# Turning the first norm's rows on VectorE in blocks of 32 by 32 instead of on TensorE

## The chip, the cores and the metric

The kernel runs on one core of one Trainium2 chip. The metric is the device time of one execution in microseconds (us), as the median over runs of the same program.

## What is computed

Batches of 256 rows by 256 features pass through two blocks, each with a residual. Cut to what matters:

```python
# x, ctx: (16, 256, 256); 8 heads of 32
q = layernorm(x); k = v = ctx                       # the "first norm"
pre = 15 * tanh((concat([q, k, v]) @ ifgate_w.T + b) / 15)
i_pre, f_pre = pre[..., :8], pre[..., 8:]
lf = cumsum(log_sigmoid(f_pre))
log_d[t, s] = lf[t] - lf[s] + i_pre[s]  (s <= t);  m = max_s log_d
s_mat = (q @ k.T / sqrt(32)) * exp(log_d - m)
h = s_mat @ v / (max(|sum s_mat|, exp(-m)) + eps);  h = h * rms_scale * gain
x = x + h
z = layernorm(x)                                    # the "second norm"
a = silu(z @ w1.T * s1) * (z @ w2.T * s2)           # 256 -> 1024
a = gelu(a @ h1.T * t1);  a = gelu(a @ h2.T * t2)   # 1024 -> 1024, twice
out = x + a @ w3.T * s3                             # 1024 -> 256
```

All is float32. The kernel writes each activation as a rounded high part plus a low part (`h_hi`, `h_lo`, type fp32r) and multiplies both by the weights, so every product is two matmuls. The same is done with the inputs of the gate product (`keys_hi/lo`, `normed_hi/lo`).

## The kernel before

The 16 batches are worked in 8 pairs; a pair is 512 rows, four tiles of 128. Each engine has its own instruction stream, written out by hand in program order, and the streams meet only at semaphores. The main loop is `batch(i, ...)`, for i = 0 to 7, on TensorE (PE), ScalarE (ACT) and VectorE (DVE). Three pairs are in flight in it: pair i is in the feed-forward block, pair j = i + 1 in the mixing block, and pair g = i + 2 in its first norm and gates. So the steps on g are done in i = 0 to 5.

One step i on PE is `swiglu` (8 groups, m = 0 to 7), hidden layer 0 (L1209/L1210, 8 groups of 16 matmuls of 512 columns), hidden layer 1 (the same) and `project` (64 matmuls of 256 columns). In a hidden layer groups m = 0 and 1 are interleaved over k = 0 to 7, since each k needs its own `lo`; `between_3(k)` runs after the k-th pair of products of layer 1, `after_3(m)` after its group m. For each group ACT does `gelu` (L591, out of PSUM into `work`) and the copy to `h_hi` (L596), and DVE does `lo` (L890), the subtraction that gives `h_lo`. A PE group waits for the gelu of four groups before it, since four PSUM banks go round.

The steps on g, in the order in which they depend on each other:

1. DVE, layer 0, m = 3 and 4: `norm_1_stats`, `norm_rsqrt`, `norm_1_apply` (L693) put the normed rows in `z` (128 partitions x 4 tiles x 256).
2. PE, layer 1, `between_3(3)`: `turn_z(g)`, 8 transposes of 128 x 128 (L1036) from `z` to `ps_a` banks 0 and 1.
3. ACT, ahead of layer 1's gelus: `split_keys(g)`, then `take_zT(g)`, which waits for the transposes and copies PSUM twice: to `zT` (L510) and, rounded, to `normed_hi` (L516).
4. POOL: `split_keys_low` (L457) and `split_normed_low` (L461) write the low parts; the second is `normed_lo = zT - normed_hi`.
5. PE, `after_3(2)`: `gates(g)`, 16 matmuls; it waits for `s_zlo`, the low part.
6. ACT after gelu 2: `take_gate_low` (L520). DVE after `lo` 2: `add_gate_low` (L736, into a part of the tile that the profile names `decay`). ACT after gelu 3: `soft_cap` (L527), then `softplus` (a table load, L535, L537; the next gelu loads its table back).
7. DVE after `lo` 3: `scan_f` (L743, L747); after `lo` 4: `scan_m` (L755, L759, L760, L761).
8. PE, `after_3(7)`, between layer 1 and `project`: `turn_rows(g)` (L1106), two transposes of `rows`, which wait for the last instruction of `scan_m`. ACT copies them out in `take_cols`.

Around them on DVE, for pair j: at the end of layer 0 `take_state`, `take_far` (L807), `take_num` (L819), which waits for `values(j, 1, 1)`, PE's matmuls of `between_3(0)`, then `mix_divide` (L830 to L833); ahead of layer 1's first `lo` come `mix_square` (L839 to L843), `mix_rsqrt`, `residual` and `norm_2_stats`; after `lo` 1 `norm_rsqrt` and `norm_2_apply`. PE turns the second norm's rows in `turn_z2(j)`, `after_3(6)`.

SP issues the loads and stores in order. `load_z(g)` waits for `s_zT` of the pair before; `keep_rows(g)` and `spread_max(g)` wait for `scan_m`. `scores(j, b)` and `read_state(j)` on PE read `zT`.

Of the kernel before, what the change touches and what calls it, by code (L numbers as in the profile page):

```python
# [15 lines left out]
P = 128  # L16
# [10 lines left out]
BACKEND_EPS, RMS_EPS, LN_EPS = 5e-05, 1e-06, 1e-05  # L27
MASKED = 1e30
RSQRT_SEED = 0x5F3759DF

W = 2
PAIRS = BATCH // W
# [39 lines left out]
def build(nc, x, ctx_tok, ctx_t, gate_w, gate_b, outnorm_w, w_cols, scales, w3_s, out):  # L72
    with ExitStack() as stack:
# [157 lines left out]
        def plain(j):  # L231

            return j < W
# [38 lines left out]
        def reuse(eng, semaphore, value):  # L272

            if not (isinstance(value, int) and value <= 0):
                eng.wait_ge(semaphore, value)
# [222 lines left out]
        def _(act):  # L498
# [8 lines left out]
            def take_zT(j):  # L507
                act.wait_ge(s_zT, j + 1)
                source = ps_f[:, 0:CH] if early(j) else ps_a[:, 0:CH]
                act.activation(zT(j), source, ACT.Copy).then_inc(s_zTe, 1)  # L510
                if plain(j):
                    return
                reuse(act, s_gate, j)
                if j >= 2:
                    act.wait_ge(s_mm, 2 * KH * (j - 2) + KH)
                act.activation(normed_hi, source, ACT.Copy).then_inc(s_zhi, 1)  # L516

            def take_gate_low(j):
                act.wait_ge(s_gate, j + 1)
# [78 lines left out]
            def batch(i, a_stage, g_stage):  # L598
                j, g = i + 1, i + 2
                for m in range(KH):  # L600
                    silu(i, m)
                    if m >= 1:
                        hi_1(i, m - 1)
                hi_1(i, KH - 1)
                if a_stage:
                    decay_cols(j)
                    for b in range(W):
                        decays(j, b)
                for m in range(KH):
                    gelu(i, 0, m)  # L610
                    if a_stage and m == 5:
                        take_near(j)
                if g_stage:
                    split_keys(g)
                    take_zT(g)
                for m in range(KH):
                    gelu(i, 1, m)
                    if g_stage and m == 2:
                        take_gate_low(g)
                    if g_stage and m == 3:  # L620
                        soft_cap(g)
                        softplus(g)
                    if g_stage and m == 7:
                        take_cols(g)
                if a_stage:
                    take_z2T(j)
# [28 lines left out]
        def _(dve):  # L655
# [49 lines left out]
            def norm_1_apply(j):  # L705
                if early(j):
                    dve.wait_ge(s_zT, j)
                norm_apply(j, xs[j] if plain(j) else z, z, s_z)

            def norm_2_stats(j, src):  # L710
                norm_stats(s_norm2, j, src)
# [215 lines left out]
            def batch(i, a_stage, g_stage, last=False):  # L927
                j, g = i + 1, i + 2
                for m in range(KH):
                    swiglu(i, m)  # L930
                    if m >= 1:
                        lo_1(i, m - 1)
                lo_1(i, KH - 1)
                if a_stage:
                    masks(j)
                    floors(j)
                    weigh_scores(j, 0)
                for m in range(KH):
                    lo(i, 0, m)
                    if a_stage and m == 1:  # L940
                        weigh_scores(j, 1)
                    if g_stage and m == 3:
                        norm_1_stats(g)
                    if g_stage and m == 4:
                        norm_rsqrt(s_norm1, g)
                        norm_1_apply(g)
                    if a_stage and m == 5:
                        take_state(j)
                    if a_stage and m == 6:
                        take_far(j)  # L950
                    if a_stage and m == 7:
                        take_num(j)
                        mix_divide(j)
                    if last:
                        compare(COMPARED_BEFORE_LAST + m)
                if a_stage:
                    mix_square(j)
                    mix_rsqrt(j)
                    residual(j)
                    norm_2_stats(j, xs[j % 2])  # L960
                for m in range(KH):
                    lo(i, 1, m)
                    if a_stage and m == 1:
                        norm_rsqrt(s_norm2, j)
                        norm_2_apply(j, xs[j % 2])
                    if g_stage and m == 2:
                        add_gate_low(g)
                    if g_stage and m == 3:
                        scan_f(g)
                    if g_stage and m == 4:  # L970
                        scan_m(g)
                    if last:
                        compare(COMPARED_BEFORE_LAST + KH + m)
                    elif a_stage and not g_stage and m >= KH - COMPARED_BEFORE_LAST:
                        compare(m - KH + COMPARED_BEFORE_LAST)
                if last:
                    sum_inexact()
                if a_stage:
                    take_z2T(j)
                finish(i)  # L980
                if last:
                    decide()
# [49 lines left out]
        def _(pe):  # L1032
# [6 lines left out]
            def turn_z(j):  # L1039
                pe.wait_ge(s_z, j + 1)  # L1040

                if j >= 2:
                    pe.wait_ge(s_num, j)
                turn(z, ps_f[:, 0:CH] if early(j) else ps_a[:, 0:CH], s_zT)
# [35 lines left out]
            def gates(j):  # L1080

                pe.wait_ge(s_gw_split, 5)
                pe.wait_ge(s_keys_lo, j - W + 1)
                pe.wait_ge(s_zTe, j + 1)

                pe.wait_ge(s_num, j)
                to = gate_out(j)[0:SPLIT_COLS]
                for b in range(W):
                    at = slice(HEADS * (1 - b), HEADS * (1 - b) + SPLIT_COLS)
                    for c in range(CH):  # L1090
                        for part in (keys_hi, keys_lo):
                            pe.matmul(to, gw_split[:, CH + c, at], part[:, c, b * SEQ:(b + 1) * SEQ],  # L1092
                                      start=(b == 0 and c == 0 and part is keys_hi), stop=False)
                pe.wait_ge(s_zlo, j - W + 1)
                for b in range(W):
                    at = slice(HEADS * (1 - b), HEADS * (1 - b) + SPLIT_COLS)
                    for c in range(CH):
                        for part in (normed_hi, normed_lo):
                            last = pe.matmul(to, gw_split[:, c, at], part[:, c, b * SEQ:(b + 1) * SEQ], start=False,  # L1099
                                             stop=(b == W - 1 and c == CH - 1 and part is normed_lo))  # L1100
                last.then_inc(s_gate, 1)
# [7 lines left out]
            def scores(j, b):  # L1109
                if b == 0:  # L1110

                    pe.wait_ge(s_zTe, j + 1)
                    pe.wait_ge(s_cols, j + 1)
                    reuse(pe, s_z2lo, j)
                    reuse(pe, s_num, j)
                    if first(j):
                        pe.wait_ge(s_gact, GATE_STEPS + 1)
                elif first(j):
                    pe.wait_ge(s_mask, MASK_STEPS)
                else:  # L1120
                    pe.wait_ge(s_smat, SMAT_STEPS * j + ROWGRP)
                for t in range(TILES):
                    for c in range(CH):
                        for r in range(ROWGRP):
                            d = slice(r * DH, (r + 1) * DH)
                            col = (c * TILES + t) * P
                            at = slice((b * TILES + t) * P, (b * TILES + t + 1) * P)
                            last = pe.matmul(score_out(j, b, r)[:, col:col + P], ctxT(j)[d, c, at], zT(j)[d, c, at], start=True, stop=True)  # L1128
                last.then_inc(s_qk, 1)
# [128 lines left out]
            def batch(i, a_stage, g_stage, as_is=False, last=False):  # L1258
# [17 lines left out]
                        read_state(j)  # L1276

                def after_3(m):
                    if g_stage and m == 2:
                        gates(g)  # L1280
                    if a_stage and m == 6:
                        turn_z2(j)
                    if g_stage and m == 7:
                        turn_rows(g)
# [10 lines left out]
                def between_3(k):  # L1295
                    if a_stage and k == 0:
                        values(j, 1, 1)
                    if g_stage and k == 3:
                        turn_z(g)

                def within_3(m):
                    pass
# [105 lines left out]
```

## Time and profile before

| | |
|---|---|
| median of 3 runs | 841.72 us (840.33 to 843.19) |
| the profiled execution's own time | 841.54 us |
| its span, first to last instruction | 839.7 us |
| busy: PE / DVE / ACT / POOL | 97% / 66% / 45% / 6% |
| mean granted TensorE clock | 0.972 |

The profile is of one execution. PE means TensorE's matmuls, PEld its weight loads, which overlap them. A time in a timeline counts from the span's start. A bracket behind a row is the idle time of that engine just before it, with what ended it. PEclk is the share of full speed at which TensorE's clock was granted.

### The profile page before, as it was taken

The page shows a single profiled execution, that of the slowest core. Times are in us where ns is not written, and L with a number is a line of the kernel's source. Part 1 is how long each engine was busy: PE and PEld are TensorE (multiplying, and loading weights), DVE is VectorE, ACT ScalarE, POOL GpSimd, SP SyncE. Part 2 cuts the span into 40 slices and gives each one's busy share as a digit, 9 for nine tenths or more (in the row PEclk, how much of TensorE's full clock was granted, in tenths as well). Part 3 has the DMA queues.
Part 4 walks back from the last instruction along what each step waited for, and adds up shares of the span by engine and source line. Part 5 has one row for each costly group of instructions (what it writes and reads, how often), then busy time and mean ns, then how long its engine had stood idle before and what let it go on. Part 6 is the DMA issues. An engine that isn't in the chain of part 4 may idle for free.

```text
span 839.7 us, 11914 instructions
## 1 busy us (share of the span) xinstructions
PE 816.1 (97%) x4666; PEld 693.7 (83%) x4666; DVE 558.1 (66%) x1335; ACT 375.9 (45%) x546; POOL 47.7 (6%) x53
## 2 busy tenths in 40 slices
PE   8895999999999999999999999999999999999996
PEld 7694788888888888888888888888888888888885
DVE  5656785758685695858666595947857583865543
ACT  2301554546345562455545462355535463336331
POOL 3100002000020001100020001100020000000000
PEclk9657999999999999999999999999999999999999
DMA  9804000040012200040002200131000300350540
GB/s 340 352 2 176 1 26 27 26 176 1 26 52 101 76 26 27 25 159 18 27 26 94 108 26 12 41 127 51 26 27 30 147 1 1 125 172 5 164 137 27
DMA packets 14027, 63.24 MB, mean 75 GB/s; under 512 B 1952, under 2 KB 2320, under 8 KB 11152
## 3 DMA queue, kind: packets, MB, share of 16 engines
q1 hardware_dynamic: 12672, 50.91, 17.4%
q0 software_dynamic: 1296, 11.53, 3.5%
q8 instruction: 38, 0.62, 0.3%
q14 instruction: 21, 0.17, 0.1%
HBM read 53.94 MB, written 8.50 MB: 74 GB/s over the span
## 4 chain that ended last, share of the span: by engine, by line
PE 78%; DVE 12%; issue 1%; ACT 1%; DVEq 0%; ACTq 0%
PE ps_f L1209 22%; PE ps_f L1210 22%; DVE decay L776 7%; PE ps_f L1185 7%; PE ps_f L1186 7%; PE ps_a L1148 6%; PE ps_f L1242 4%; PE ps_f L1243 4%; DVE decay L792 2%; PE ps_a L1128 2%; PE ps_a L1036 2%; PE ps_a L1137 1%; PE ps_a L1158 1%; PE ps_a L1099 1%; PE ps_a L1092 1%
## 5 line engine op out<-in xcount | busy, mean ns | idle before, releaser
L1209 PE MATMUL ps_f<-h_hi,wgt 128*128 128x512 f32 x1024 | 404.1, 395 | 0.0
L1210 PE MATMUL ps_f<-h_lo,wgt 128*128 128x512 f32 x1024 | 399.1, 390 | 0.0
L1209 PEld LDWEIGHTS ps_f<-h_hi,wgt 128*128 128x128 f32 x1024 | 192.4, 188 | 40.3 <-issue 0.5
L1210 PEld LDWEIGHTS ps_f<-h_lo,wgt 128*128 128x128 f32 x1024 | 192.4, 188 | 38.0
L890 DVE TENSOR_TENSOR h_lo<-work,h_hi 128x512 fp32r<-128x512 f32 x128 | 86.5, 690 | 135.0 <-ACT h_hi L596 134.0
L591 ACT ACTIVATE work<-ps_f,scl 128x512 f32<-128x512 f32 x128 | 87.5, 683 | 161.4 <-PE ps_f L1210 161.2
L1185 PE MATMUL ps_f<-h_hi,wgt 128*128 128x512 f32 x256 | 101.4, 396 | 0.1
L1186 PE MATMUL ps_f<-h_lo,wgt 128*128 128x512 f32 x256 | 100.4, 392 | 0.0
L578 ACT ACTIVATE work<-ps_f,scl 128x512 f32<-128x512 f32 x64 | 44.1, 688 | 92.6 <-PE ps_f L1186 92.6
L596 ACT ACTIVATE h_hi<-work 128x512 fp32r<-128x512 f32 x128 | 80.9, 632 | 4.0
L881 DVE SCALAR_TENSOR_TENSOR work<-ps_f,scl,work 128x512 f32<-128x512 f32 x64 | 48.1, 751 | 49.2 <-ACT work L578 49.2
L776 DVE SCALAR_TENSOR_TENSOR decay<-decay,cols,future 128x128 f32<-128x128 f32 x224 | 64.5, 364 | 0.0
L1242 PE MATMUL ps_f<-wgt,h_hi 128*128 128x256 f32 x256 | 62.2, 285 | 0.0
L1148 PEld LDWEIGHTS ps_a<-v_aug,decay 128*128 128x128 f32 x480 | 60.7, 201 | 1.6
L1243 PE MATMUL ps_f<-wgt,h_lo 128*128 128x256 f32 x256 | 61.8, 283 | 0.0
L1185 PEld LDWEIGHTS ps_f<-h_hi,wgt 128*128 128x128 f32 x256 | 48.0, 188 | 15.1 <-DVE work L881 3.7
L1148 PE MATMUL ps_a<-v_aug,decay 128*128 128x33 f32 x480 | 59.1, 280 | 0.0
L1186 PEld LDWEIGHTS ps_f<-h_lo,wgt 128*128 128x128 f32 x256 | 48.1, 188 | 8.8
L557 ACT ACTIVATE decay<-decay 128x1024 f32<-128x1024 f32 x32 | 33.9, 1060 | 42.8 <-DVE decay L776 42.8
L1243 PEld LDWEIGHTS ps_f<-wgt,h_lo 128*128 128x128 f32 x256 | 49.1, 192 | 0.1
L1242 PEld LDWEIGHTS ps_f<-wgt,h_hi 128*128 128x128 f32 x256 | 49.1, 192 | 0.1
L886 DVE TENSOR_TENSOR h_lo<-work,h_hi 128x512 fp32r<-128x512 f32 x64 | 43.7, 683 | 0.8
(156 smaller groups left out, 764.5 us busy)
## 6 DMA issues: line engine op xcount, KB each, us to landing
decay<-m_rows SPq DMA_DIRECT2D x14, 1024.0 KB, 6.1
decay<-w_cols SPq DMA_DIRECT2D x22, 512.0 KB, 4.2
wgt<-w_cols POOLq DMA_DIRECT2D x5, 1024.0 KB, 13.7
v_aug<-ctx_tok SPq DMA_DIRECT2D x8, 528.0 KB, 3.6
xs<-x SPq DMA_DIRECT2D x8, 512.0 KB, 3.6
wgt<-w_cols POOLq DMA_DIRECT2D x2, 2048.0 KB, 10.0
x_kept<-xs SPq DMA_DIRECT2D x8, 512.0 KB, 2.7
out<-xs SPq DMA_DIRECT2D x8, 512.0 KB, 2.6
```

Of the source, the lines that this page charges most:

```text
L591: act.activation(work[:, m % GELU], ps_f[:, (turn_of(i) + m) % 4], ACT.Gelu, scale=scl[:, 2 + layer, m:m + 1]).then_inc(s_gelu, 1)
L596: act.activation(h_hi[1 - layer][:, m], work[:, m % GELU], ACT.Copy).then_inc(s_hi, 1)
L776: last = dve.scalar_tensor_tensor(part, maxima, cols[:, t, row:row + 1], future[:], ALU.subtract, ALU.add)
L881: dve.scalar_tensor_tensor(work[:, 2 + m % 2], ps_f[:, bank], scl[:, 1, m:m + 1], work[:, m % 2], ALU.mult, ALU.mult).then_inc(s_hf, 1)
L890: dve.tensor_tensor(h_lo[1 - layer][:, m], work[:, m % GELU], h_hi[1 - layer][:, m].bitcast(F32), ALU.subtract).then_inc(s_lo, 1)
L1148: last = pe.matmul(value_out(j, b, t)[:, h * DV:(h + 1) * DV], decay_of(b, h, t), v_aug[:, b * TILES + t, h, :], start=True, stop=True)
L1185: pe.matmul(ps_f[:, bank + half], w, moving(z2_hi[:, c], as_is), start=(c == 0), stop=False)
L1186: last = pe.matmul(ps_f[:, bank + half], w, moving(z2_lo[:, c], as_is), start=False, stop=(c == CH - 1))
L1209: pe.matmul(ps_f[:, bank], w, moving(h_hi[layer][:, k], as_is), start=(k == 0), stop=False)
L1210: last = pe.matmul(ps_f[:, bank], w, moving(h_lo[layer][:, k], as_is), start=False, stop=(k == KH - 1))
L1242: pe.matmul(to, moving(h_hi[0][:, k, q * P:(q + 1) * P], as_is), w, start=(k == 0), stop=False)
L1243: last = pe.matmul(to, moving(h_lo[0][:, k, q * P:(q + 1) * P], as_is), w, start=False, stop=(k == KH - 1))
```

## The change

For the pairs g = 2 to 7 (batches 4 to 15) the transposes leave PE. DVE turns `z` into `zT` itself, in 16 instructions for each pair, each of 32 partitions by 256 columns (8 blocks of 32 x 32), from partitions 32g.. to partitions 32o.., in two halves of 8. The first half stands after `take_far` (layer 0, m = 6), the second after `mix_divide` (m = 7); the last one signals `s_zT`. The copy to `zT` on ACT goes. The rounded copy `normed_hi` is made by the new `split_normed` from `zT` in SBUF, after gelu 1 of layer 1. `gates`, `take_gate_low`, `add_gate_low`, `soft_cap` with `softplus`, `scan_f` and `scan_m` all stand one group later than before. `turn_rows` and `turn_z2` stay where they were. Pairs 0 and 1 are turned on PE as before.

```diff
@@ scalar @@
                 act.activation(zT(j), source, ACT.Copy).then_inc(s_zTe, 1)
-                if plain(j):
-                    return
-                reuse(act, s_gate, j)
-                if j >= 2:
-                    act.wait_ge(s_mm, 2 * KH * (j - 2) + KH)
-                act.activation(normed_hi, source, ACT.Copy).then_inc(s_zhi, 1)
+
+            def split_normed(j):
+                act.wait_ge(s_zT, j + 1)
+                act.wait_ge(s_gate, j)
+                act.wait_ge(s_mm, 2 * KH * (j - 2) + KH)
+                act.activation(normed_hi, zT(j), ACT.Copy).then_inc(s_zhi, 1)
...
                 if g_stage:
                     split_keys(g)
-                    take_zT(g)
                 for m in range(KH):
                     gelu(i, 1, m)
-                    if g_stage and m == 2:
+                    if g_stage and m == 1:
+                        split_normed(g)
+                    if g_stage and m == 3:
                         take_gate_low(g)
-                    if g_stage and m == 3:
+                    if g_stage and m == 4:
                         soft_cap(g)
                         softplus(g)
@@ vector @@
+            def turn_z(j, part):
+
+                dve.wait_ge(s_z, j + 1)
+                dve.wait_ge(s_far, j)
+                for g in range(2 * part, 2 * part + 2):
+                    for o in range(P // BLOCK):
+                        src = z[g * BLOCK:(g + 1) * BLOCK].rearrange("p q (c o d) -> p o c q d", c=CH, d=BLOCK)[:, o]
+                        dst = zT_buf[o * BLOCK:(o + 1) * BLOCK].rearrange("p c (q g d) -> p g c q d", g=P // BLOCK, d=BLOCK)[:, g]
+                        last = dve.transpose(dst, src)
+                if part:
+                    last.then_inc(s_zT, 1)
...
                     if a_stage and m == 6:
                         take_far(j)
+                    if g_stage and m == 6:
+                        turn_z(g, 0)
                     if a_stage and m == 7:
                         take_num(j)
                         mix_divide(j)
+                    if g_stage and m == 7:
+                        turn_z(g, 1)
...
-                    if g_stage and m == 2:
+                    if g_stage and m == 3:
                         add_gate_low(g)
-                    if g_stage and m == 3:
+                    if g_stage and m == 4:
                         scan_f(g)
-                    if g_stage and m == 4:
+                    if g_stage and m == 5:
                         scan_m(g)
@@ tensor @@ (in gates, and in scores for g >= 2)
-                pe.wait_ge(s_zTe, j + 1)
+                pe.wait_ge(s_zT, j + 1)
...
                 def after_3(m):
-                    if g_stage and m == 2:
+                    if g_stage and m == 3:
                         gates(g)
...
                 def between_3(k):
                     if a_stage and k == 0:
                         values(j, 1, 1)
-                    if g_stage and k == 3:
-                        turn_z(g)
```

## Rows read from the trace of the kernel before

**Rows 1.** The page: engines by busy time; the chain that ended last.

```profile
PE 816.1 (97%) x4666; PEld 693.7 (83%) x4666; DVE 558.1 (66%) x1335; ACT 375.9 (45%) x546; POOL 47.7 (6%) x53
...
PE 78%; DVE 12%; issue 1%; ACT 1%; DVEq 0%; ACTq 0%
```

**Rows 2.** Timeline of PE at a turn: start us, us, engine, line, operation.

```profile
139.86 0.39 PE L1209 MATMUL ps_f<-h_hi,wgt 128*128 128x512 f32 x1
140.09 0.40 PE L1210 MATMUL ps_f<-h_lo,wgt 128*128 128x512 f32 x1
140.33 1.04 PE L1036 MATMUL ps_a<-ident,z 128*128 128x128 f32 x8
...
141.43 0.39 PE L1210 MATMUL ps_f<-h_lo,wgt 128*128 128x512 f32 x1
```

**Rows 3.** Groups by line: xcount | busy us, mean ns | idle before.

```profile
L890 DVE TENSOR_TENSOR h_lo<-work,h_hi 128x512 fp32r<-128x512 f32 x128 | 86.5, 690 | 135.0 <-ACT h_hi L596 134.0
...
L839 DVE TENSOR_TENSOR decay<-num 128x1024 f32<-128x1024 f32 x8 | 9.8, 1225 | 0.3
...
L693 DVE TENSOR_SCALAR z<-z,mv,nw 128x256 f32<-128x256 f32 x24 | 8.3, 408 | 0.2
...
L743 DVE TENSOR_TENSOR_SCAN state<-state 16x256 f32<-16x256 f32 x7 | 4.7, 678 | 17.2 <-ACT state L537 17.2
```

**Rows 4.** Timeline of DVE: how closely 256-column instructions follow one another.

```profile
123.34 1.38 DVE L693 TENSOR_SCALAR z<-z,mv,nw 128x256 f32<-128x256 f32 x4
```

**Rows 5.** Timeline of DVE, first batch step: [idle before <-releaser].

```profile
130.68 0.70 DVE L807 TENSOR_TENSOR state<-ps_a,e_cols 128x528 f32<-128x528 f32 x1
136.43 0.69 DVE L890 TENSOR_TENSOR h_lo<-work,h_hi 128x512 fp32r<-128x512 f32 x1 [5.05 <-ACT h_hi L596]
137.74 0.71 DVE L819 TENSOR_TENSOR num<-ps_a,state 128x528 f32<-128x528 f32 x1 [0.62 <-PE ps_a L1148]
...
140.55 1.23 DVE L839 TENSOR_TENSOR decay<-num 128x1024 f32<-128x1024 f32 x1
...
159.24 0.69 DVE L890 TENSOR_TENSOR h_lo<-work,h_hi 128x512 fp32r<-128x512 f32 x1
159.85 0.41 DVE L736 TENSOR_TENSOR decay<-ps_a,decay 48x256 f32<-48x256 f32 x1
160.18 0.67 DVE L890 TENSOR_TENSOR h_lo<-work,h_hi 128x512 fp32r<-128x512 f32 x1
...
167.06 0.42 DVE L759 TENSOR_TENSOR rows<-state 16x256 f32<-16x256 f32 x1
167.50 0.28 DVE L760 TENSOR_SCALAR rows<-rows,state 16x128 f32<-16x128 f32 x1
167.71 0.28 DVE L761 TENSOR_SCALAR rows<-state 16x128 f32<-16x128 f32 x1
```

**Rows 6.** Timeline of ACT in the same step.

```profile
144.62 0.69 ACT L591 ACTIVATE work<-ps_f,scl 128x512 f32<-128x512 f32 x1 [1.28 <-PE ps_f L1210]
...
154.21 0.69 ACT L591 ACTIVATE work<-ps_f,scl 128x512 f32<-128x512 f32 x1 [3.26 <-PE ps_f L1210]
...
160.29 0.51 ACT L527 ACTIVATE rows<-decay,gb 48x256 f32<-48x256 f32 x1 [4.72 <-DVE decay L736]
```

**Rows 7.** Timeline of PE in the same step: the gate columns' transposes.

```profile
169.42 0.30 PE L1106 MATMUL ps_a<-ident,rows 80*128 80x80 f32 x2
```

**Rows 8.** Instructions of DVE L843: duration ns min/median/max, first and last start.

```profile
L843 DVE TENSOR_SCALAR rms<-rms x8: 181/2335/2341, 64.0 to 719.8; 128x32 f32<-128x32 f32 x8
```

**Rows 9.** Timeline of POOL in the same step.

```profile
143.42 2.40 POOL L461 TENSOR_TENSOR h_lo<-zT,h_hi 128x1024 fp32r<-128x1024 f32 x1 [3.59 <-ACT h_hi L516]
```

**Rows 10.** Timeline of PE at its longest idle time.

```profile
76.38 1.97 PE L1036 MATMUL ps_a<-ident,num 128*128 128x128 f32 x8 [9.95 <-DVE num L693]
```

**Rows 11.** Stretches around it: PE, PEld, DVE, ACT, POOL, PEclk, DMA, GB/s.

```profile
69.00:70.00 1.00, 0.00 (x0) 0.00 (x0) 0.97 (x2) 0.00 (x0) 0.00 (x0) 0.69 1.01 419
...
79.00:80.00 1.00, 1.00 (x8) 1.00 (x8) 0.43 (x1) 0.98 (x2) 0.00 (x0) 0.69 0.00 0
```

More of the change, by code:

```diff
@@ L29 @@
 RSQRT_SEED = 0x5F3759DF
+BLOCK = 32
 W = 2
@@ L1110, in scores @@
                 if b == 0:
-                    pe.wait_ge(s_zTe, j + 1)
+                    if plain(j):
+                        pe.wait_ge(s_zTe, j + 1)
+                    else:
+                        pe.wait_ge(s_zT, j + 1)
                     pe.wait_ge(s_cols, j + 1)
```

## The prediction

> **What bounds the kernel now.** I read the page first: PE is busy 97% of the span, DVE 66%, ACT 45%, and the chain that ended last runs 78% on PE and 12% on DVE [rows 1]. The reader should take from this that matmul time removed from PE comes off the end, and that the second engine which can set the end is DVE, over stretches where its own program order makes it late. So the question is local: where PE meets DVE after the change. For that I read one step, i = 0, in the timelines of PE, DVE, ACT and POOL. The steps i = 1 to 5 repeat it to 0.1 us, and the sum is one step times 6.
>
> In layer 1 of that step PE never waits. DVE does: from 137.74, where `take_num` (L819) is released by PE, to the end of L890 at 160.18 + 0.67, it has no idle time in front of any instruction but for gaps of 0.05 us between linked ones [rows 5]. That is 23 us of DVE work in one piece, released by PE at its head. At its end hang `add_gate_low` (L736, 159.85), on which ACT's `soft_cap` waited 4.72 us [rows 6], then softplus, both scans, and at last L761, which ends at 167.71 + 0.28 = 167.99 [rows 5]. PE needs that row for `turn_rows`, which it started at 169.42 [rows 7]. The slack of this whole chain is 169.42 - 167.99 = 1.43 us. It is the number on which the case turns.
>
> **The change part by part.**
>
> *PE's transposes go.* Matmuls of layer 1 follow one another every 0.23 us (139.86 to 140.09). With the turn between them, the second matmul after 140.09 starts at 141.43 in place of 140.55 [rows 2]. The gain is 0.88 us a step, 5.3 us in six steps. It is on the path, since PE is the path. It also brings PE to `turn_rows` 0.88 us sooner, at 168.54, so the slack falls to 0.55.
>
> *DVE's 16 transposes.* No row shows one. The nearest rows are 128 x 256 instructions with one tensor input, L693: 0.408 us each [rows 3], and four in 1.38 us [rows 4], which makes (1.38 - 0.408) / 3 = 0.324 us from start to start. That rate holds where an instruction may start before the one ahead has finished. Rows 5 show both cases at `scan_m`: L760 and L761 write the same partitions (from 64 up), and L761 starts 0.21 us after L760, of whose 0.28 us 0.07 are still to run. L759 writes from partition 32 up and L760 from 64, with no wait between them in the code, and there L760 starts 0.44 us after L759, whose time is 0.42: nothing overlaps. Each of the 16 transposes writes another 32 partitions than the one before. So I price one as a full duration plus 0.02, 0.408 + 0.02 = 0.43, and take T = 0.45 for the block order, of which no row tells. Lower end 0.324, if they overlap; upper end 0.70, if they are as slow for 256 columns as the scan L743 with 0.678 us [rows 3].
>
> The Trainium skill ("VectorE: DVE Perf Modes", section "Two Vector instructions with no wait between them") says that a Vector instruction whose input or output starts in another quadrant than the last one's is held until all before it have finished. The trace agrees, with the 0.44 against 0.21 us above. By this rule all the transposes are held and T is at least 0.43; without it the sum would go with 0.324 and come out 6 us lower.
>
> *The first half*, 8T = 3.6 us, stands after L807 (130.68 + 0.70), where DVE idles 5.05 us before the next `lo` [rows 5]. It costs nothing up to T = 0.63; above that it delays `lo` 7, which PE needs only at k = 7, several us later.
>
> *The second half* stands after `mix_divide`, inside the 23 us piece. Nothing hides it: everything from L839 (140.55) on is 8T = 3.6 us later.
>
> *The gate steps stand one group later.* `gates` meets no new wait: PE gets there with group 3, whose gelu starts at 154.21 [rows 6] after the old gates' matmuls, so the new ones begin at about 151.4; `split_normed` follows two gelus from 144.62 - 0.88 on at some 1.26 us each, so it begins at 146.3 and ends at 147.3, and POOL's subtraction of 2.40 us [rows 9] ends at 149.8. On DVE one more `lo` is now in front of `add_gate_low`, which takes 0.61 us of its queue (159.24 to 159.85) [rows 5]. From the end of L736 (160.26) to the end of L761 (167.99) the chain is as before, 7.73 us, with gelu and `lo` 5 in the places of 4. So the whole chain ends at 167.99 + 0.61 + 8T = 168.60 + 8T.
>
> *PE at `turn_rows`.* It waits for that. The hand-over costs at least the 0.03 us seen from DVE to ACT (160.26 to 160.29, rows 5 and 6), and PE starts again from standstill, at most the 0.30 us that both transposes take [rows 7]; I take 0.2 for both. All that follows on PE (project, the next step) hangs on this start and has no other lateness: project's first products need `lo` 4 and 5, done by then, its last ones `lo` 7, which comes 1.3 us after the scan with 3.4 us of products ahead of it. `turn_z2` needs L693 of the second norm, which ends by 159.24 + 8T = 162.8, before PE's 164.0; it would stall above T = 0.6. SP's `keep_rows` and `spread_max` go later by the same 3 us and are wanted only in the next step, over 20 us on.
>
> *ACT's copy* (1.03 us) and the copy from SBUF in place of PSUM lie in ACT's idle time; ACT waits for PE before gelu 0 [rows 6]. Worth nothing.
>
> *POOL and DVE meet again.* L843, on 128 x 32, takes 0.181 us at least and 2.335 in the median [rows 8]: in this step it starts with POOL's 2.40 us subtraction and ends with it (143.42 + 2.40) [rows 9]. That blocks the 23 us piece for 2.15 us. The subtraction now runs from 147.4 to 149.8, and DVE, 3.6 us late and not yet blocked, is then between L843 and `mix_rsqrt`. I count the same 2.15 us again, no change.
>
> **The sum.** New start of `turn_rows` less the old one: 168.60 + 8T + 0.2 - 169.42 = 8T - 0.62. With T = 0.45 that is 2.98 us a step (a stall of 3.86 less the 0.88 gained), in six steps 17.9. The profiled execution took 841.54 us (a span of 839.7 and 1.84 around it); the sum gives it 859.4. The median of the runs is 0.18 higher: 859.6. With T = 0.324 it is 853.6; with 0.70, 4.98 a step, 871.6.
>
> **The rivals.**
>
> 1. *The clock falls in the stall.* PE's longest idle time, 9.95 us up to 76.38 [rows 10], began at 66.43. The clock was full at first and at half (1.2 GHz of 2.4) from about 69.4, since 69 to 70 has a mean of 0.69; by the same reckoning it was full again at about 79.6 [rows 11], 3.2 us after PE's restart. My stall of 3.86 us is longer than the 3.0 us of idle time after which it fell. Against it: before that idle time PE had done thin work, here dense matmuls. Price: 3.2 us at half rate lose 1.6 us a step, 9.6 in six: 869.1; if some stalls escape, 861 to 868.
>
> 2. *Slow transposes.* T = 0.55 to 0.70: 864 to 872, and then with rival 1 behind it up to 880. For it: four-byte elements, and 32-element runs in both patterns. The Trainium skill ("VectorE: DVE Perf Modes", "The three transpose paths" and "Rules for kernel authors") speaks against this change: it says to transpose 128 x 128 on TensorE if PSUM will do, and gives VectorE 311 ns for 128 columns of two bytes. An estimate from this, twice that for 256 columns, 0.62 us, would make the sum 868. No run here shows it.
>
> 3. *The block by POOL drops out*, the one that could end on the other side. Place: L843. If POOL's subtraction now falls on instructions that it does not hold up, 2.15 us come back, and a step is worth 8T - 2.77. It decides from T = 0.345 down: at 0.324, 840.6; at 0.27 (256 columns at the 1.045 ns a column that lie between L890 and L839 [rows 3]) 838. At T = 0.45 it gives 846.7. Against: the shift leaves DVE among instructions of the same kinds.
>
> 4. *DVE's half is covered after all*, because the real slack is larger than I read: then only PE's gain stays, 836.4. Against: not one idle row between L819 and L736.
>
> **How the numbers follow.** The likeliest case (T between 0.40 and 0.50, clock full) 0.59, range 857 to 862. Rival 1 0.18. Rival 2 0.08. Overlapping transposes (853 to 857) 0.05. Rival 3 0.06, mostly at 845 to 848 and a third of it at or under 841. Rival 4 0.04. The prediction is 859.5. From 852 to 870 lie the first two, the overlapping case and a little of rival 2, about 0.83. A measurement of this kernel can tell about 0.3% (2.5 us) from no change. Faster has rival 4 and the lowest part of rival 3, 0.05; the same 0.03; slower the rest, 0.92.
>
> **What the changed profile would show.** PE: no L1036 on `z` after the first 20 us, and idle time in front of the gate columns' transposes, about 3.9 us, six times, with DVE `rows` as releaser. DVE: 96 transposes, busy 0.41 to 0.45 us each and no closer than that from start to start; the first half inside idle time; from `mix_square` to `add_gate_low` no idle time. POOL's block of about 2.2 us on an instruction of `mix_rsqrt`. PEclk full in layer 1 and in project, else rival 1. The prediction is wrong if PE does not wait before `turn_rows`, if it waits at another place (`gates` on `s_zlo`, `turn_z2`), or if a transpose takes well under 0.35 or over 0.55 us.

## The result

| | before | after |
|---|---|---|
| median device time, 6 runs each | 842.64 us (840.33 to 844.07) | 869.25 us (867.53 to 870.75) |
| profiled execution: time / span | 841.54 / 839.7 us | 869.2 / 865.2 us |
| mean granted TensorE clock | 0.972 | 0.962 |

The changed kernel is slower: ratio 1.0318, 95% interval 1.0298 to 1.0338. Its time lies inside the forecast range of 852 to 870, but 9.75 us above the forecast 859.5 and outside the 857 to 862 of the likeliest case. It is almost on the 869.1 of the rival with the falling clock.

**The profile after.** The page's busy line and its chain that ended last, by engine:

```profile
PE 818.6 (95%) x4618; PEld 695.4 (80%) x4618; DVE 600.0 (69%) x1431; ACT 370.7 (43%) x540; POOL 47.7 (6%) x53
...
PE 54%; DVE 31%; ACT 4%; issue 3%; DVEq 0%; ACTq 0%
```

PE fell from 78% to 54% of the chain, DVE rose from 12% to 31% [rows 1 for before]. One group of the lines shows the new instructions:

```profile
L720 DVE STREAM_TRANSPOSE zT<-z 32x256 f32<-32x256 f32 x96 | 41.9, 436 | 2.0
```

The timeline of DVE in the first step, answering to [rows 5]:

```profile
131.21 3.58 DVE L720 STREAM_TRANSPOSE zT<-z 32x256 f32<-32x256 f32 x8
136.16 0.69 DVE L904 TENSOR_TENSOR h_lo<-work,h_hi 128x512 fp32r<-128x512 f32 x1 [1.37 <-ACT h_hi L597]
137.47 0.71 DVE L833 TENSOR_TENSOR num<-ps_a,state 128x528 f32<-128x528 f32 x1 [0.62 <-PE ps_a L1169]
...
140.27 3.59 DVE L720 STREAM_TRANSPOSE zT<-z 32x256 f32<-32x256 f32 x8
143.90 1.23 DVE L853 TENSOR_TENSOR decay<-num 128x1024 f32<-128x1024 f32 x1
...
146.86 0.18 DVE L857 TENSOR_SCALAR rms<-rms 128x32 f32<-128x32 f32 x1
147.08 2.40 DVE L669 TENSOR_SCALAR rms<-rms 128x32 int32<-128x32 int32 x1
149.52 0.18 DVE L670 TENSOR_SCALAR rms<-rms 128x32 int32<-128x32 int32 x1
...
162.64 1.29 DVE L904 TENSOR_TENSOR h_lo<-work,h_hi 128x512 fp32r<-128x512 f32 x2
163.85 0.41 DVE L750 TENSOR_TENSOR decay<-ps_a,decay 48x256 f32<-48x256 f32 x1
164.19 0.67 DVE L904 TENSOR_TENSOR h_lo<-work,h_hi 128x512 fp32r<-128x512 f32 x1
...
171.71 0.27 DVE L775 TENSOR_SCALAR rows<-state 16x128 f32<-16x128 f32 x1
```

The 7.17 us of transposes stand as forecast: the first eight in idle time (5.05 us before, 1.37 left), the second eight in front of L853, the old L839. From start to start they take (3.59 - 0.436) / 7 = 0.45 us. Down to L750, the old L736, there is no idle time. L669 takes 2.40 us: it is now the instruction that POOL's subtraction (147.04 to 149.44) blocks, where before it was L843. The chain ends at 171.71 + 0.27 = 171.98.

PE in the same step, answering to [rows 7], with its idle time in the bracket; then the same wait of all six steps together (us in all, times, mean us):

```profile
172.03 0.53 PE L1124 MATMUL ps_a<-ident,rows 80*128 80x80 f32 x2 [3.66 <-DVE rows L775]
```

```profile
PE ps_a L1124 <- DVE rows L775: 21.9, 6, 3.7
```

The stall is there, 3.66 us, released by DVE's last row of `scan_m`, and 21.9 us in six steps. What it costs a step is read from something that happens once a step. POOL's first instruction of a step (start us, us) serves; two rows of before, and five of after:

```profile
101.17 1.39 POOL L452 TENSOR_TENSOR num<-v_aug,e_cols 128x256 f32<-128x256 f32 x2 [73.69 <-ACT e_cols L550]
...
678.54 1.40 POOL L452 TENSOR_TENSOR num<-v_aug,e_cols 128x256 f32<-128x256 f32 x2 [51.57 <-ACT e_cols L550]
```

```profile
100.89 1.39 POOL L453 TENSOR_TENSOR num<-v_aug,e_cols 128x256 f32<-128x256 f32 x2 [73.72 <-ACT e_cols L551]
...
202.62 1.40 POOL L453 TENSOR_TENSOR num<-v_aug,e_cols 128x256 f32<-128x256 f32 x2 [53.18 <-ACT e_cols L551]
...
504.48 1.40 POOL L453 TENSOR_TENSOR num<-v_aug,e_cols 128x256 f32<-128x256 f32 x2 [52.11 <-ACT e_cols L551]
...
603.64 1.39 POOL L453 TENSOR_TENSOR num<-v_aug,e_cols 128x256 f32<-128x256 f32 x2 [50.61 <-ACT e_cols L551]
...
704.31 1.40 POOL L453 TENSOR_TENSOR num<-v_aug,e_cols 128x256 f32<-128x256 f32 x2 [52.12 <-ACT e_cols L551]
```

A step took (678.54 - 101.17) / 6 = 96.23 us before. Now the first takes 101.73, the fifth 99.16, and the other four 100.55 to 100.67. The fifth is the pure cost of the stall: 99.16 - 96.23 = 2.93 us, a stall of 3.66 and its restart less the transposes saved. The rest shows in the clock. Stretches of the stall of the first step, of the 4 us behind it and of the one in which the clock rises again, and of the 4 us behind the stall of the fifth (PE, PEld, DVE, ACT, POOL, then PEclk):

```profile
168.40:172.00 3.60, 0.00 (x0) 0.00 (x0) 2.17 (x5) 3.50 (x6) 0.00 (x0) 0.88 0.01 3
172.00:176.00 4.00, 3.97 (x19) 3.97 (x20) 2.52 (x3) 2.62 (x4) 0.00 (x0) 0.50 0.65 235
177.33:178.33 1.00, 1.00 (x8) 1.00 (x7) 0.00 (x0) 0.00 (x0) 0.00 (x0) 0.69 0.97 410
575.90:579.90 4.00, 4.00 (x36) 4.00 (x35) 2.21 (x3) 2.51 (x3) 0.00 (x0) 1.00 0.75 309
```

Behind the first stall the clock is at half (1.2 GHz of 2.4) up to about 178.0, and PE gets 19 matmuls into 4 us; behind the fifth it is full, and it gets 36. So the account of the 27.7 us between the two profiled executions is: 6 x 2.93 = 17.6 for the stalls; 101.73 - 99.16 = 2.6 in the first step and 1.4 to 1.5 in four more, 8.5 in all, for the clock; and 2.1 in the time around the span, 4.0 in place of 1.84. These make 28.2; the 0.5 too much is made up at the start and the end (the first step begins 0.28 us earlier than before, and what follows the last one is 0.27 us shorter). (The medians are 26.6 apart.)

### The profile page after: what moved, and what is told of

It reads as the page before. It is cut to its first block, busy times and chain, and to the rows that moved or that the text cites. A ratio compares the mean times of both kernels' runs of the same rounds, so it can differ in the third digit from the quotient of the medians.

```text
span 865.2 us, 11914 instructions
## 1 busy us (share of the span) xinstructions
PE 818.6 (95%) x4618; PEld 695.4 (80%) x4618; DVE 600.0 (69%) x1431; ACT 370.7 (43%) x540; POOL 47.7 (6%) x53
## 4 chain that ended last, share of the span: by engine, by line
PE 54%; DVE 31%; ACT 4%; issue 3%; DVEq 0%; ACTq 0%
PE ps_f L1230 12%; PE ps_f L1231 11%; DVE decay L790 7%; PE ps_f L1206 7%; PE ps_f L1207 7%; PE ps_a L1169 6%; PE ps_f L1263 4%; PE ps_f L1264 4%; DVE zT L720 2%; DVE h_lo L904 2%; DVE decay L806 2%; PE ps_a L1149 2%; DVE rms L669 2%; DVE stats L680 1%; DVE num L870 1%
## 5 line engine op out<-in xcount | busy, mean ns | idle before, releaser
L904 DVE TENSOR_TENSOR h_lo<-work,h_hi 128x512 fp32r<-128x512 f32 x128 | 85.9, 689 | 102.7 <-ACT h_hi L597 101.6
L1263 PE MATMUL ps_f<-wgt,h_hi 128*128 128x256 f32 x256 | 69.8, 307 | 0.0
L1264 PE MATMUL ps_f<-wgt,h_lo 128*128 128x256 f32 x256 | 68.9, 304 | 0.0
L1263 PEld LDWEIGHTS ps_f<-wgt,h_hi 128*128 128x128 f32 x256 | 55.2, 216 | 0.1
L1264 PEld LDWEIGHTS ps_f<-wgt,h_lo 128*128 128x128 f32 x256 | 55.0, 215 | 0.1
```

Of the source, the lines that this page charges most:

```text
L904: dve.tensor_tensor(h_lo[1 - layer][:, m], work[:, m % GELU], h_hi[1 - layer][:, m].bitcast(F32), ALU.subtract).then_inc(s_lo, 1)
L1263: pe.matmul(to, moving(h_hi[0][:, k, q * P:(q + 1) * P], as_is), w, start=(k == 0), stop=False)
L1264: last = pe.matmul(to, moving(h_lo[0][:, k, q * P:(q + 1) * P], as_is), w, start=False, stop=(k == KH - 1))
```

## The experiments

Each is compared with the kernel before on the same chip, whose median there was 841.25 to 841.57 us. What is said of stalls, steps and the clock is read from the one profiled execution of each kernel. Steps are the surer measure: the first step of the profiled executions began anywhere from 99.6 to 104.7 us, with mean clocks of 0.74 to 0.81 up to there, and that moves the whole time.

**1. The stall filled with work, twice.** In PE's stream, behind the last group of layer 1:

```diff
                     if g_stage and m == 7:
+                        for _ in range(36):
+                            pe.matmul(ps_a[:, 3, 0:P], ident[:], ident[:], start=True, stop=True)
                         turn_rows(g)
```

> The changed kernel with 36 more products of 128 x 128 on the identity, into a PSUM bank that is free then, between layer 1's last group and the gate columns' transposes; their results are not used. Theory (the extra time is a stall of 3.65 us in front of these transposes, 2.93 us net a step, plus TensorE at half clock for some 3 us after five of six stalls, 1.5 to 2.5 us each): the chain on VectorE is as late as before, but the clock stays full, so 842.6 + 6 x 2.93 = 860 to 861. Rival (the clock falls for another reason, such as the sparse weight loads of project): 869. Rival (the filling itself holds the transposes up): above 862 with a full clock.

Measured: 884.64 us, ratio 1.0514 (1.0498 to 1.0531), a miss. I had sized the products wrongly: the 36 take 8.03 us, 0.223 each, more than the stall, and hold the transposes up. So the run came out as the rival for filling said. The clock stayed full in all steps, though, which are all 103.38 us: 96.23 - 0.88 + 8.03 = 103.38. The second try had 15 products.

> As stall_filled, with 15 products in place of 36: one took 0.223 us there, so 15 take 3.35 us, less than the stall of 3.65. Theory (the clock falls for the stall): steps of 96.23 + 2.93 = 99.2 us, all six with a full clock, 842 + 17.6 = 860. Rival (the clock falls for another reason): 869, steps of 100.6.

Measured: 858.53 us, ratio 1.0208 (1.0187 to 1.0230), 10.7 us under the changed kernel. PE's timeline and the clock of the 4 us behind the stalls of steps 1 and 2:

```profile
168.38 3.51 PE L1306 MATMUL ps_a<-ident 128*128 128x128 f32 x30
172.19 0.36 PE L1124 MATMUL ps_a<-ident,rows 80*128 80x80 f32 x2 [0.30 <-DVE rows L775]
```

```profile
172.20:176.20 4.00, 4.00 (x34) 4.00 (x35) 2.48 (x3) 2.58 (x4) 0.00 (x0) 1.00 0.65 263
271.40:275.40 4.00, 4.00 (x34) 4.00 (x35) 2.47 (x3) 2.56 (x4) 0.00 (x0) 1.00 0.67 230
```

The transposes still wait for DVE, now 0.30 us behind the products; all six steps take 99.1 to 99.2 us, the 2.93 again, and the clock is full. The chain's lateness and the clock's fall are thus two costs, and the second comes from the idle time: with products in its place it is gone. Of the 10.7 us, 2.1 are the time around the span, 1.9 us here; see experiment 6.

**2. The second half left out.**

```diff
-                if part:
+                if not part:
                     last.then_inc(s_zT, 1)
...
-                    if g_stage and m == 7:
-                        turn_z(g, 1)
```

> The changed kernel without the second half of VectorE's transposes, so that half of the turned rows is left as it was. Theory (only the second half lies on the chain to the gate columns): the chain ends 3.6 us sooner, TensorE stalls 0.1 to 0.3 us a step, its clock stays full, and the gain of the removed transposes stays: 842.6 - 6 x 0.6 = 838 to 840. Rival (the later places of gates and scans cost by themselves, by one group or 3.6 us): 850 or more. Rival (the first half costs too): over 845.

Measured: 839.05 us, ratio 0.9965 (0.9952 to 0.9979). PE no longer idles in front of the gate columns for more than 0.1 us, and a step takes 95.42 us, 0.81 less than before: most of the saved transposes. So the first half costs nothing by itself, and the later places of the gate steps at most 0.1 us: their 0.61 us stand against a slack of 0.55, the weight load of L1122 waits 0.30 us, and steps without any wait take 95.31 (experiment 5). All that a step loses comes through the second half, and with it (experiment 4) the 0.61 us of the later places. That the median is only 2.2 us below the kernel before, and not 6 x 0.81, is mostly the time around the span (experiment 6).

**3. Transposes within their own 32 partitions.** Number and size are the same:

```diff
-                        dst = zT_buf[o * BLOCK:(o + 1) * BLOCK].rearrange(...)[:, g]
+                        dst = zT_buf[g * BLOCK:(g + 1) * BLOCK].rearrange(...)[:, o]
```

> The changed kernel with each block turned within its own 32 partitions, so that four transposes in a row read and write the same partitions; the blocks land in other places than they should. Theory (a transpose waits for the one before it when its partitions start elsewhere, by the trace and the Trainium skill, VectorE: DVE Perf Modes): six of eight follow at about 0.33 us, one half takes 2.8 to 2.9 us in place of 3.59, and the stall before the gate columns is 2.9 in place of 3.65 us: 869.3 - 4.4 = 865, and down to 857 if the shorter stall keeps the clock full more often. Rival (transposes never overlap): a half stays at 3.59 us and the time at 869.

Measured: 860.34 us, ratio 1.0217 (1.0196 to 1.0238). The two halves in DVE's timeline, and its group (duration ns min/median/max), to be compared with L720 above:

```profile
132.00 2.84 DVE L720 STREAM_TRANSPOSE zT<-z 32x256 f32<-32x256 f32 x8
...
141.06 2.86 DVE L720 STREAM_TRANSPOSE zT<-z 32x256 f32<-32x256 f32 x8
```

```profile
L720 DVE STREAM_TRANSPOSE zT<-z x96: 390/394/443, 132.0 to 640.8; 32x256 f32<-32x256 f32 x96
```

A half takes 2.86 us in place of 3.59: (2.84 - 0.39) / 7 = 0.35 us from start to start in place of 0.45, with one change of partitions still among the seven. The stall falls by 0.87 to 2.79 us: 0.73 from the shorter half, the rest from POOL's block, which now costs 2.28 us on L674 and not 2.40 on L669. The Trainium skill (VectorE: DVE Perf Modes, "Two Vector instructions with no wait between them") says that a change of quadrant holds an instruction back until all before it are done; the trace agrees, 0.45 against 0.35 us. Steps took 98.32 us where the clock stayed full (2.09 above before, 0.84 under the changed kernel's), but three of the six were 99.7 to 99.8 and one 101.06: idle time of 2.79 us brought the clock down in four of six cases. The profiled execution, 863.65 us, was the slowest of the four. Two others took 858.7 us, with a mean clock of 0.971 against its 0.963, which fits a clock that fell less often in them, and with it a median 5 us under the 865 expected; they were not profiled, so this is not shown.

**4. Both halves in the gap, and the gate steps back.** Two ways to shorten the chain, each alone. First:

```diff
                     if g_stage and m == 6:
                         turn_z(g, 0)
+                        turn_z(g, 1)
...
-                    if g_stage and m == 7:
-                        turn_z(g, 1)
```

> The changed kernel with both halves of the transposes ahead of layer 0's last subtraction, where VectorE idled 4.95 us. Theory: 7.2 us in a gap of 4.95 make the chain 2.25 us late, of which 0.62 were idle anyway, so 1.6 us in place of 3.6: the stall before the gate columns falls to 1.65 us, net 0.95 a step, the clock stays full: 842.6 + 5.7 = 848 to 849. Rival (the whole length of the transposes counts wherever they stand): 860 or more. Rival (clock falls also after short stalls): 857.

Measured: 847.11 us, ratio 1.0073 (1.0055 to 1.0091). DVE and PE:

```profile
129.93 7.19 DVE L720 STREAM_TRANSPOSE zT<-z 32x256 f32<-32x256 f32 x16
137.15 1.67 DVE L904 TENSOR_TENSOR h_lo<-work,h_hi 128x512 fp32r<-128x512 f32 x1
138.75 0.69 DVE L833 TENSOR_TENSOR num<-ps_a,state 128x528 f32<-128x528 f32 x1
```

```profile
168.51 0.36 PE L1123 MATMUL ps_a<-ident,rows 80*128 80x80 f32 x2 [1.42 <-DVE rows L775]
```

The 16 transposes take 7.19 us where 5.05 were idle, the stall falls to 1.42 us, a step takes 96.95 (0.72 above before), and the clock stays full. L904 takes 1.67 us, not 0.69, as POOL's subtraction for the keys now blocks it; the `mix_divide` instruction that it blocked before is free in exchange.

Second, the gate steps on their old places (likewise `add_gate_low` at 2, `soft_cap` at 3, `scan_f` at 3, `scan_m` at 4):

```diff
                     split_keys(g)
+                    split_normed(g)
...
-                    if g_stage and m == 1:
-                        split_normed(g)
-                    if g_stage and m == 3:
+                    if g_stage and m == 2:
                         take_gate_low(g)
...
-                    if g_stage and m == 3:
+                    if g_stage and m == 2:
                         gates(g)
```

> The changed kernel with the gate steps on their old places, one group sooner, and the rounded copy ahead of layer 1's gelus. Theory, two terms: one subtraction less in front of the gate sum, 0.61 us; and GpSimd's subtraction now runs from 145.0 to 147.5, of which the first 1.2 us lie under a reduction on VectorE that reads one operand and is not held up, so that the block falls from 2.2 to about 1.15 us. The stall is 3.65 - 0.61 - 1.1 = 1.9 us, net 1.2 a step, clock full: 842 + 7 = 849. Rival (the block stays 2.2 us wherever the subtraction falls): stall 3.0, net 2.3, 842 + 14 = 856, up to 865 if the clock falls. Rival (TensorE now waits at the gates for the low part): idle time there, over 860.

Measured: 853.97 us, ratio 1.0147 (1.0130 to 1.0165). The profiled execution was the fastest of the five, 849.71 us, with a full clock behind its stalls of 1.7 to 2.1 us. DVE and POOL in its first step:

```profile
144.12 1.23 DVE L852 TENSOR_TENSOR decay<-num 128x1024 f32<-128x1024 f32 x1
145.38 1.22 DVE L853 TENSOR_REDUCE rms<-decay 128x32 f32<-128x1024 f32 x1
146.63 1.08 DVE L854 TENSOR_TENSOR rms<-rms,den 128x32 f32<-128x32 f32 x1
147.75 0.19 DVE L855 SCALAR_TENSOR_TENSOR rms<-rms,den 128x32 f32<-128x32 f32 x1
```

```profile
145.26 2.40 POOL L462 TENSOR_TENSOR h_lo<-zT,h_hi 128x1024 fp32r<-128x1024 f32 x1 [5.48 <-ACT h_hi L517]
```

POOL's 2.40 us start under the reduction L853, which takes its usual 1.22 us, and only L854 behind it is stretched, to 1.08 us. So 0.89 us are lost in place of 2.22, and the chain is 0.61 sooner besides; together 1.94, and the stall of this step fell from 3.66 to 1.70. A step is 1.0 us above before in five of six. For the profiled execution that is the theory's 849; the median is 5 us above it. The other four runs are 852.9 to 859.2 us, at mean clocks of 0.960 to 0.967 against 0.971. A clock that falls after some of these shorter stalls too would fit, but they were not profiled, so this is not shown.

**5. The change without its stall.** Both halves in the gap as in 4, and DVE's chain shortened where it waited 2.15 us for ScalarE between the gate sum and the first scan. The second norm's inverse root and application (3.6 us) go there:

```diff
-                    if a_stage and m == 1:
-                        norm_rsqrt(s_norm2, j)
-                        norm_2_apply(j, xs[j % 2])
                     if g_stage and m == 3:
                         add_gate_low(g)
+                    if a_stage and m == (3 if g_stage else 1):
+                        norm_rsqrt(s_norm2, j)
+                        norm_2_apply(j, xs[j % 2])
```

> Both halves of the transposes in the gap ahead of layer 0's last subtraction, and the second norm's inverse root and its application moved from behind subtraction 1 of layer 1 to behind the gate sum, where VectorE waited 2.15 us for ScalarE. Theory: the chain of both_in_gap ends 2 us sooner, TensorE stalls nowhere by more than 0.1 us, and only its saved transposes remain: steps of 95.35 to 95.5 us, 842 - 5 = 837. Rival (the second norm's rows now come too late for their own transposes on TensorE, which need them by 163.7): the stall moves there, 840 to 845.

> As gap_norm_later, with the gate steps on their old places too. Theory: 0.61 us more slack on the chain, which is worth nothing if there was no stall left: 837, the same as gap_norm_later. Rival (TensorE waits at the gates for the low part, or GpSimd's two subtractions, now back to back, hold VectorE up longer): 839 to 845.

(this one is the first with the diff of gates_back, the norm's steps behind the gate sum at m = 2)

> The kernel before with only the move of the second norm's inverse root and application behind the gate sum. Theory (the gain of gap_norm_later is TensorE's saved transposes, since before there was no stall to remove): steps of 96.2 us, 841.5 as before. Rival (the move itself is the gain): 839 or less.

(the diff above at m = 2 in the kernel before)

Measured: gap_norm_later 838.94 us, ratio 0.9970 (0.9960 to 0.9980); gap_norm_gates 839.08 us, 0.9968 (0.9955 to 0.9982); before_norm_later 842.20 us, 1.0000 (0.9989 to 1.0012). In both of the first two PE waits nowhere in the steps, the gate columns' transposes included. A step takes 95.31 us in gap_norm_later and 95.33 in gap_norm_gates, 0.92 and 0.90 less than before. POOL's first instruction of a step in gap_norm_later, for (674.45 - 102.62) / 6 = 95.31:

```profile
102.62 1.40 POOL L453 TENSOR_TENSOR num<-v_aug,e_cols 128x256 f32<-128x256 f32 x2 [75.16 <-ACT e_cols L551]
...
674.45 1.40 POOL L453 TENSOR_TENSOR num<-v_aug,e_cols 128x256 f32<-128x256 f32 x2 [46.74 <-ACT e_cols L551]
```

That is the whole of the transposes' 0.88. The times are 2 us above the expected 837, which is the time around the span (experiment 6). The move of the norm by itself is worth nothing, since before there was no stall for it to remove.

**6. The time around the span.** The device time less the span is 1.8 to 2.0 us in every run of the kernel before, of before_norm_later and of the two filled kernels, and 3.8 to 4.5 us in every run of the changed kernel and of experiments 2 to 5 built from it. The first have at least as many instructions in PE's stream as before, the others 96 fewer. So I put 96 waits that wait for nothing into PE's 10 us of idle time before the first turn of the second norm:

```diff
             keep_clock(24, 1)
+            for _ in range(96):
+                pe.wait_ge(s_ident, 5)
             turn_z2(0)
```

> gap_norm_later with 96 redundant waits in TensorE's stream, in its idle time before the first pair's second norm is turned; they take the place in number of the 48 transposes and 48 weight loads that the change removed. What they test: the device time lies 1.9 us above the span in the kernel before and in both kernels with filled stalls, and 3.8 to 4.5 us above it in every kernel with fewer TensorE instructions than before. Theory (it hangs on the length of TensorE's stream): 1.9 us again, 837. Rival (it hangs on something else, as VectorE's transposes or what ends last): 4 us, 839.

> The changed kernel with the same 96 redundant waits and nothing else. Theory: 1.9 us between span and device time in place of 4.0, and 867 in place of 869.3. Rival: 4.0 and 869.3.

Measured: gap_norm_padded 835.79 us, ratio 0.9924 (0.9910 to 0.9938), with 1.9 to 2.0 us around the span in all six runs. after_padded 869.12 us, 1.0312 (1.0293 to 1.0331): 1.9 to 2.0 us around the span in all four, as expected, but no shorter in total, which was not expected. The steps of its profiled execution are 101.92 and 100.61 to 101.86 us: there the clock fell in all six of them, and that took back more than the padding gave. The other three were not profiled; their spans are 865.7 to 867.6 us at mean clocks of 0.958 to 0.960, against 863.6 to 866.8 at 0.958 to 0.964 for the changed kernel. What in the stream makes the 2 us, its length or something else, was not found.

**7. Holding the clock in PE's long idle time.** 40 products of 16 columns at the same place:

```diff
             keep_clock(24, 1)
+            for _ in range(40):
+                pe.matmul(ps_f[:, 1, 0:16], ident[:], ident[:, 0:16], start=True, stop=True)
             turn_z2(0)
```

> gap_norm_later with 40 short products (16 columns) in TensorE's 10 us of idle time ahead of the first turn of the second norm, so that the clock does not fall there. Theory: the clock stays full from 62 us on, turn and first products run at full speed, 1 to 2 us less than gap_norm_later, and with more TensorE instructions the time outside the span is 1.9: 835 to 836. Rival (the short products leave the clock low, or delay the turn): 839 or more.

Measured: 841.28 us, ratio 0.9994 (0.9984 to 1.0004): a miss. Stretches over these products:

```profile
64.00:66.00 2.00, 2.00 (x21) 2.00 (x20) 1.73 (x9) 0.00 (x0) 0.00 (x0) 1.00 0.95 393
66.00:68.00 2.00, 2.00 (x19) 2.00 (x18) 1.97 (x2) 0.00 (x0) 0.00 (x0) 0.91 1.05 434
68.00:70.00 2.00, 2.00 (x11) 2.00 (x11) 1.93 (x4) 0.00 (x0) 0.00 (x0) 0.50 0.90 368
```

```profile
64.76 14.46 PE L1368 MATMUL ps_f<-ident 128*128 128x16 f32 x80
```

The clock falls at about 67.6 us although PE has these products without a gap. They last 14.5 us, most of it at half clock. DVE had the rows for the turn ready at 75.02, and PE came to it at 79.06, 4.0 us later. These products held PE up and did not hold the clock. More TensorE instructions did give 1.9 us around the span again.

## Why the prediction came out as it did

- *The chain and its slack.* Right. 1.43 us of slack, eaten by the second half of the transposes and one `lo`. The step begins 0.28 us earlier in the trace after than in the one before, so its end of the chain, 171.98, stands for 172.26; forecast 168.60 + 3.6 = 172.20.
- *T = 0.45 us.* Measured 0.45, and 0.436 for each, where the nearest row gave 0.408. The exact hit is in part luck: the price from the rows was 0.43, and the last 0.02 had no row. Rival 2 (0.55 to 0.70, with its estimate of 0.62) did not come true. The step from "nothing overlaps between L759 and L760" to "the transposes do not overlap" was tested in experiment 3.
- *The first half free, the gate steps free in themselves, ACT's copy worth nothing.* Right to 0.1 us a step; experiment 2 shows the three together.
- *POOL's block counted the same.* Right, 2.22 us lost in place of 2.15, on L669, an instruction of `mix_rsqrt`, as written. The rival in which it drops out did not come true here; experiment 4 shows that more than half of it (1.33 of 2.22 us) does when the subtraction falls under the reduction.
- *The sum a step.* Forecast 2.98, measured 2.93 (stall 3.66, forecast 3.86; the 0.2 us for hand-over and restart were mostly in the restart). Over six steps 17.6 of 17.9.
- *"Clock full"*, in the likeliest case. Wrong, and this is the step that failed. I weighed dense matmuls before the stall against the idle time before which PE had done thin work, and gave the clock's fall 0.18. It fell after five of six stalls of 3.65 us. The rival's price, 1.6 us a step, was right for four of them (1.4 to 1.5); the first cost 2.6, as the clock fell 0.9 us before the restart and stayed at half for 5.9 us behind it, and the fifth nothing. Experiment 1 shows that it was the idle time that brought it down. The argument against the rival was weak in the trace before already: PE ran products of 128 columns without a gap right up to its long idle time, with a full clock over their last 4 us, and the clock fell all the same.

```profile
59.33 7.11 PE L1316 MATMUL ps_f<-ident 128*128 128x128 f32 x48
```

- *"1.84 around it", carried over unchanged.* The term was missing 2.1 us, and no rival had it. Experiments 6 and 7 show that more instructions in PE's stream bring the 1.9 us back with all of VectorE's transposes in place; why is open.

With both, 859.6 + 8.5 + 2.1 = 870.2; less 0.3 for the stalls and 0.5 at the start and end, 869.4, and 869.25 was measured. That the time is almost on the rival's 869.1 is thus partly luck: its 9.6 us for the clock were 8.5, and 2.1 us that it did not have came from around the span.

The gain that the change could have had, 0.88 us a step, is real and is paid out once nothing waits: 842 to 836 us in gap_norm_padded.

## What to carry to other kernels

Work taken off the engine that is the bound helps only if the engine that takes it over has slack on every chain that the first one waits for; count the slack at the next meeting point (here 1.43 us), not by busy shares (DVE was 66% busy). A wait of TensorE can cost more than its length, since the clock may fall behind it: here 1.4 to 2.6 us more in five of six waits of 3.65 us. A wait that must stay was cheaper filled with products of 128 columns than left empty, as long as they were shorter than the wait: 15 took 10.7 us off the changed kernel (2.1 of them around the span), 36 added 15.4. Before giving up such a move, look for idle time on the receiving engine's own queue: two moves within VectorE's order turned 3.2% slower into 0.3% faster, and 0.8% with TensorE's stream padded.

## What the runs showed of the hardware

- Idle time of TensorE of 3.65 us brought the clock to half in five of six cases (in all six of after_padded), of 2.79 us in four of six, of 1.7 to 2.1 us (gates_back) and of 1.42 us in none; each count is of one profiled execution. In some cases it fell only after the restart: in the changed kernel's third step some 1.5 us behind it.
- 40 products of 16 columns, back to back, did not hold the clock: it fell some 3 us after they had begun.
- A VectorE transpose of 32 x 256 float32 took 0.436 us and 0.45 from start to start when the written partitions changed, and 0.39 and 0.35 when they mostly stayed.
- GpSimd's two-operand subtraction (2.40 us) held up VectorE's instructions with two operands in SBUF and its small `tensor_scalar` ones, but not a reduction with one (1.22 us, unchanged).
- With 96 fewer instructions in TensorE's stream the device time lay 3.8 to 4.5 us above the span in place of 1.8 to 2.0. 96 waits that do nothing brought it back.
